# Logits in another bank, experts picked across a change of set, sums behind a tile: a two-layer expert FFN on one core

## The reference

```python
# first layer, one LoRA expert for each sequence
hidden_i = x @ wi.T + 2 * (x @ common_wi_a.T) @ common_wi_b.T + expert_lora(x, ids, wi_a, wi_b)
hidden_i = relu(hidden_i)
hidden_o = hidden_i @ wo.T + 2 * (hidden_i @ common_wo_a.T) @ common_wo_b.T + expert_lora(hidden_i, ids, wo_a, wo_b)
# second layer: the router looks at the mean over all tokens of a sequence
probs = softmax(hidden_o.mean(axis=1) @ gate_w)
top_w, top_i = top_k(probs, 2); top_w /= top_w.sum()
for e in range(8):
    y = gelu(hidden_o @ w1[e] + b1[e]) @ w2[e] + b2[e]
    out += combine[:, e] * y          # combine is top_w at top_i, else 0
return x + out
```

## Time and profile before

| what | us |
|---|---|
| median of three runs | 271.2 (271.2 to 271.35) |
| the profiled execution | 271.83 |
| its span, first to last instruction | 270.0 |
| TensorE busy | 262.4 |
| VectorE busy | 174.9 |
| ScalarE busy | 174.3 |
| GpSimd busy | 159.8 |

### The profile page before, as it was taken

The page is one execution under the profiler, slowest core; times in us unless marked ns, Lnnn a source line. Parts: engine busy times, 40 slices in busy tenths (PEclk is TensorE's granted clock), DMA queues, the critical chain, the costliest instruction groups (busy, mean ns, idle before and its releaser), DMA issues.

```text
span 270.0 us, 3606 instructions
## 1 busy us (share of the span) xinstructions
PE 262.4 (97%) x1150; PEld 211.8 (78%) x1150; DVE 174.9 (65%) x283; ACT 174.3 (65%) x279; POOL 159.8 (59%) x192
## 2 busy tenths in 40 slices
PE   7999999999979999999999999999999999999995
PEld 3668888887757888888888788888788888888883
DVE  1784767374699645657595696566865667665664
ACT  2747464554725459987986887677676776775650
POOL 2166998943666687799619999466356366331100
PEclk9999999999999999999999999999999999999999
DMA  5995120201023022112201122202012015000004
GB/s 183 350 385 187 39 78 0 83 1 39 0 71 111 16 78 78 21 60 78 80 1 27 51 78 80 64 13 81 24 56 78 33 47 195 0 0 2 0 1 155
DMA packets 11139, 19.76 MB, mean 73 GB/s; under 512 B 2000, under 2 KB 2256, under 8 KB 10992
## 3 DMA queue, kind: packets, MB, share of 16 engines
q1 hardware_dynamic: 10544, 18.61, 20.8%
q10 hardware_dynamic: 576, 0.92, 1.0%
HBM read 17.43 MB, written 2.10 MB: 72 GB/s over the span
## 4 chain that ended last, share of the span: by engine, by line
PE 90%; DVE 4%; issue 2%; ACT 1%; DMA 1%; SPq 1%; DVEq 0%; ACTq 0%
PE out_ps L732 15%; PE out_ps L733 15%; PE out_ps L736 15%; PE hid_ps L732 14%; PE hid_ps L733 13%; PE hid_ps L736 13%; DMA lora_first<-in_early 1%; PE hid_ps L776 1%; DVE hid_lo L1015 1%; PE hid_ps L772 1%; PE out_ps L850 1%; SPq L301 1%; ACT act_hi L628 1%; PE hid_ps L780 1%; DVE up_raw L999 1%
## 5 line engine op out<-in xcount | busy, mean ns | idle before, releaser
L406 POOL TENSOR_TENSOR up_lo<-up_raw,up_hi 128x512 fp32r<-128x512 f32 x41 | 53.0, 1312 | 41.9 <-ACT up_hi L559 41.7
L732 PE MATMUL out_ps<-hid_hi,down_hi 128*128 128x512 f32 x192 | 74.9, 390 | 0.0
L736 PE MATMUL out_ps<-hid_hi,down_lo 128*128 128x512 f32 x192 | 74.8, 389 | 0.0
L733 PE MATMUL out_ps<-hid_lo,down_hi 128*128 128x512 f32 x192 | 74.8, 389 | 0.0
L732 PE MATMUL hid_ps<-act_hi,up_hi 128*128 128x512 f32 x166 | 65.1, 392 | 0.5 <-DVE hid_lo L1015 0.3
L733 PE MATMUL hid_ps<-act_lo,up_hi 128*128 128x512 f32 x166 | 64.7, 390 | 0.0
L736 PE MATMUL hid_ps<-act_hi,up_lo 128*128 128x512 f32 x166 | 64.7, 390 | 0.0
L591 ACT ACTIVATE hid_ps<-hid_ps,bias_sb 128x512 f32<-128x512 f32 x64 | 42.2, 659 | 29.7 <-DVE hid_ps L1041 19.1
L1015 DVE SCALAR_TENSOR_TENSOR hid_lo<-hid_ps,mix,hid_hi 128x512 fp32r<-128x512 f32 x64 | 47.8, 747 | 18.7 <-ACT hid_hi L605 18.2
L412 POOL TENSOR_TENSOR down_lo<-down_raw,down_hi 128x512 fp32r<-128x512 f32 x24 | 32.1, 1338 | 41.5 <-ACT down_hi L569 41.3
L605 ACT ACTIVATE hid_hi<-hid_ps,mix 128x512 fp32r<-128x512 f32 x64 | 44.1, 689 | 4.6
(11 more groups left out here) (91 smaller groups left out, 236.3 us busy)
## 6 DMA issues: line engine op xcount, KB each, us to landing
up_raw<-in_w SPq DMA_DIRECT2D x16, 256.0 KB, 2.8
down_raw<-in_w SPq DMA_DIRECT2D x16, 256.0 KB, 2.6
lora_raw<-in_lora SPq DMA_DIRECT2D x10, 256.0 KB, 5.4
down_raw<-in_woT SPq DMA_DIRECT2D x8, 256.0 KB, 3.1
up_raw<-in_wiT SPq DMA_DIRECT2D x7, 256.0 KB, 3.8
outT<-x_sb SPq DMA_DIRECT2D x6, 256.0 KB, 3.3
x_sb<-in_xT SPq DMA_DIRECT2D x1, 1024.0 KB, 8.6
x_sb<-in_xT SPq DMA_DIRECT2D x1, 512.0 KB, 5.8
```

The costliest lines, as they stand in the source:

```text
L406: ins = eng.tensor_tensor(up_lo[:, n, cols], up_raw[:, n, cols], f32(up_hi[:, n, cols]), ALU.subtract)
L732: eng.matmul(out, w_h, a_h, start=start, stop=False, skip_group_check=onto)
L733: eng.matmul(out, w_h, a_l, start=False, stop=False, skip_group_check=onto)
L736: return eng.matmul(out, w_l, a_h, start=False, stop=stop, skip_group_check=onto)
```

## The change

No instruction is added or dropped on TensorE, and its order stays. What changes is where others stand, and which waits stand ahead of the logits:

- The logits of sequence 0 (set 5) go to bank 1 of `hid_ps` instead of bank 0. Bank 1 is free once `second_sum` has read it (`s_r2`); bank 0 was free once `hid_low(5, 0)` was done.
- `term_high` stands ahead of `hid_high(q, 0)`, and GpSimd makes the terms ahead of `lora_low(1, 4)`.
- `router_max` follows the reading of the logits at once, and `router_exp` stands in the middle of set 5.
- `router_softmax` and `router_first` come at the end of set 5, ahead of `hid_low(5, 3)`; `router_second` comes behind that.
- GpSimd waits in set 6 for both experts (`s_pick`) before it goes on; the four `token_sum` of sequence 0 move from set 5 to set 6, two ahead of `up_low(7)` and two behind, and `down_low(6)` behind them.
- `raw_high` moves from set 5 into set 6, behind `hid_high(6, 0)`; the two `sum_high` are put on either side of `hid_high(6, 2)`.

```diff
-    FIRST_AT = {6: 0, 11: 1}
+    FIRST_AT = {5: 0, 11: 1}
     SECOND_AT = {6: 0, 11: 1}
+    LOGITS_BANK = {5: 1, 10: 0}
...
@@ GpSimd
                 elif q == 4:
                     up_low(5)
                     down_low(4)
-                    after((s_down_lo, 5))
+                elif q == 5:
+                    logit_terms(0)
+                    term_low(0)
+                    after((s_term_lo, 1))
                     lora_low(1, 4)
-                elif q < N_COND - 1:
-                    if q in TOTAL_AT:
-                        logit_terms(TOTAL_AT[q])
-                        term_low(TOTAL_AT[q])
-                    up_low(q + 1)
-                    down_low(q)
-                    token_sums(q)
+                    up_low(6)
+                    down_low(5)
+                elif q == 6:
+
+                    eng.wait_ge(s_pick, TOP_K)
+                    token_sum(1, 0)
+                    token_sum(1, 1)
+                    up_low(7)
+                    token_sum(1, 2)
+                    token_sum(1, 3)
+                    down_low(6)
@@ ScalarE
                 if cond(q):
-                    hid_high(q, 0)
                     if q in LOGITS_AT:
                         term_high(LOGITS_AT[q])
+                    hid_high(q, 0)
+                    if q in EXP_AT:
+                        router_exp(EXP_AT[q])
...
+                    elif q == 6:
+                        raw_high(1, 0)
+                        raw_high(1, 1)
+                        up_high(7)
+                        hid_high(6, 1)
+                        down_high(6)
+                        sum_high(1, 0)
+                        hid_high(6, 2)
+                        sum_high(1, 1)
@@ TensorE, bank_free and router_logits
-                if bank == 0 and q - 1 in LOGITS_AT:
+                if q - 1 in LOGITS_AT and bank == LOGITS_BANK[q - 1]:
                     eng.wait_ge(s_read, LOGITS_AT[q - 1] + 1)
...
-                b = LOGITS_AT[q]
-                if b == 0:
+                b, bank = LOGITS_AT[q], LOGITS_BANK[q]
+
+                if bank == 0:
+                    eng.wait_ge(s_hid_lo, 4 * q + 1)
+                else:
                     eng.wait_ge(s_ones, 1)
-                eng.wait_ge(s_hid_lo, 4 * q + 1)
+                    eng.wait_ge(s_r2, sevens_before(q) + 1)
                 eng.wait_ge(s_term_hi, b + 1)
@@ VectorE
                     if q in LOGITS_AT:
-                        router_start(LOGITS_AT[q])
+
+                        router_start(q)
+                        router_max(LOGITS_AT[q])
                     tile_sum(q, 1)
                     for to in UP_FACTOR_AT.get(q, ()):
                         merge_up(to, hid_ps[:, 0, :])
                     tile_sum(q, 2)
-                    if q in LOGITS_AT:
-                        router_max(LOGITS_AT[q])
                     hid_low(q, 1)
                     merge_down(q, hid_ps[:, 0, :])
                     tile_sum(q, 3)
                     hid_low(q, 2)
+                    if q in FIRST_AT:
+                        router_softmax(FIRST_AT[q])
+                        router_first(FIRST_AT[q])
                     continue
                 if q > 1:
                     hid_low(q - 1, 3)
-                if q in FIRST_AT:
-                    router_softmax(FIRST_AT[q])
-                    router_first(FIRST_AT[q])
-                    router_second(FIRST_AT[q])
+                if q in SECOND_AT:
+                    router_second(SECOND_AT[q])
```

More of the change, by code:

```diff
@@ L107, in build @@
     EXP_AT = {5: 0, 11: 1}
-    FIRST_AT = {6: 0, 11: 1}
+    FIRST_AT = {5: 0, 11: 1}
     SECOND_AT = {6: 0, 11: 1}
+    LOGITS_BANK = {5: 1, 10: 0}
     MIX_B2_AT = {13: 0, 20: 1}
     READY_SEQ = [1, 0, 1]
-    RAW_HI_AT = {1: [(0, 0), (0, 1)], 5: [(1, 0), (1, 1)], 9: [(2, 0)], 10: [(2, 1)]}
+    RAW_HI_AT = {1: [(0, 0), (0, 1)], 9: [(2, 0)], 10: [(2, 1)]}
     RAW_LO_AT = {2: [(0, 0), (0, 1), (0, 2), (0, 3)], 6: [(1, 0), (1, 1), (1, 2), (1, 3)],
                  11: [(2, 0), (2, 1)], 12: [(2, 2), (2, 3)]}
-    SUM_AT = {1: [(0, 0), (0, 1)], 2: [(0, 2), (0, 3)], 5: [(1, 0), (1, 1), (1, 2), (1, 3)], 9: [(2, 0), (2, 1)], 10: [(2, 2), (2, 3)]}
-    SUM_HI_AT = {2: [(0, 0), (0, 1)], 6: [(1, 0), (1, 1)], 12: [(2, 0)], 13: [(2, 1)]}
+    SUM_AT = {1: [(0, 0), (0, 1)], 2: [(0, 2), (0, 3)], 9: [(2, 0), (2, 1)], 10: [(2, 2), (2, 3)]}
+    SUM_HI_AT = {2: [(0, 0), (0, 1)], 12: [(2, 0)], 13: [(2, 1)]}
     SUM_LO_AT = {3: [(0, 0), (0, 1), (0, 2), (0, 3)], 7: [(1, 0), (1, 1), (1, 2), (1, 3)], 13: [(2, 0), (2, 1)], 14: [(2, 2), (2, 3)]}
@@ L701, in _ @@
                         up_high(q + 2)
-                    if q in EXP_AT:
-                        router_exp(EXP_AT[q])
                     others(q)
@@ L884, in next_up_factor @@
                     eng.wait_ge(*free)
-                    if q in LOGITS_AT and seven(q):
-                        eng.wait_ge(s_read, LOGITS_AT[q] + 1)
                     up_factor(to, bank[:, 0:SW], bank[:, SW:2 * SW])
@@ L906, in router_logits @@
                     return
-                b = LOGITS_AT[q]
-                if b == 0:
+                b, bank = LOGITS_AT[q], LOGITS_BANK[q]
+                if bank == 0:
+                    eng.wait_ge(s_hid_lo, 4 * q + 1)
+                else:
                     eng.wait_ge(s_ones, 1)
-                eng.wait_ge(s_hid_lo, 4 * q + 1)
+                    eng.wait_ge(s_r2, sevens_before(q) + 1)
                 eng.wait_ge(s_term_hi, b + 1)
-                eng.matmul(hid_ps[:, 0, 0:KD * E], ones[:, :], term_hi[:, :, :].rearrange("p k e -> p (k e)"),
+                eng.matmul(hid_ps[:, bank, 0:KD * E], ones[:, :], term_hi[:, :, :].rearrange("p k e -> p (k e)"),
                            start=True, stop=True)
                 eng.wait_ge(s_term_lo, b + 1)
-                eng.matmul(hid_ps[:, 0, KD * E:2 * KD * E], ones[:, :], term_lo[:, :, :].rearrange("p k e -> p (k e)"),
+                eng.matmul(hid_ps[:, bank, KD * E:2 * KD * E], ones[:, :], term_lo[:, :, :].rearrange("p k e -> p (k e)"),
                            start=True, stop=True).then_inc(s_logit, 1)
@@ L1059, in _, with router_start @@
             max1, key1, max2, key2, inv, pair, inv_pair = (small[:, i:i + 1] for i in range(7))
-            def router_start(b):
+            def router_start(q):
+                b, bank = LOGITS_AT[q], LOGITS_BANK[q]
                 eng.wait_ge(s_logit, b + 1)
@@ L1064, in router_start @@
                     eng.wait_ge(s_exp, b)
-                eng.tensor_reduce(logit[:, :], hid_ps[:, 0, 0:2 * KD * E].rearrange("p (g e) -> p e g", e=E),
+                eng.tensor_reduce(logit[:, :], hid_ps[:, bank, 0:2 * KD * E].rearrange("p (g e) -> p e g", e=E),
                                   AX_X, ALU.add).then_inc(s_read, 1)
```

## The result

| | before | changed | ratio, 95% interval |
|---|---|---|---|
| median, six runs each, us | 271.61 (271.2 to 272.77) | 268.67 (267.93 to 269.93) | 0.9889 (0.9858 to 0.992) |
| profiled execution: span, us | 270.0 | 268.1 | |

The forecast was 268.1 us from 271.2, a ratio of 0.9886. The measured ratio is 0.9889, so the change takes 1.1% off, about 2.9 us of 271.6.

The account below looks back on a forecast made before the run. TensorE, busy 97% of the span, was taken as the bound, with four stalls of 3.30 us. Gains 0.40+0.71+1.80+0.39-0.15=3.15 us take the median from 271.2 to 268.1 us, range 267.6 to 269.5.

Parts of the forecast that it names:

- four stalls: TensorE, sets 5 and 6: before logits 0.40, up factor 0.71, down factor 1.80, tile 3 of set 6 0.39; together 3.30 us.
- Logits: Set 5: in bank 1 the logits no longer wait for hid_low(5,0), so TensorE gains 0.40 us.
- The cover of `router_max`: VectorE, set 5: the first tile sum waits for TensorE anyway, hiding router_max; without that, up to 0.6 us on VectorE.
- First expert and `hid_low(5,3)`: End of set 5: prob waits to 72.04, hid_low(5,3) ends at 73.55; the 0.71 us stall before set 7's up factor goes.
- the prediction's clock: Times in the profile before, run with the new order; the changed profile's times are 1.28 us later by its late start.
- The 0.2 to spare: Up factor of set 7: hid_low(5,3) ends at 73.55, TensorE comes at 73.80, leaving 0.2 us.
- Second expert: Set 6: picked without contention, merge_up(7) runs 74.6 to 75.3, wanted at 76.78; the 1.80 us stall goes.
- Merge of the down factor: VectorE, set 6: merge ends at 79.7, TensorE asks at 79.77; 0.15 us of the 0.39 before tile 3 stays.
- rival 1: Set 6: VectorE loses the shared port twice; stall 1.4 us instead of 0.15 before tile 3, 269.3 us; chance 0.15.
- the sign named for rival 1: Second mix or the raw_low after it over 1.2 us long, and a 1.4 us gap before tile 3 of set 6.
- Sums: Sets 6 to 8: sums' low parts come later but stay hidden; last act_lo ends near 92.0, about 1.8 us before set 8.
- Rival 3: Set 8 starts late, waiting for the sums' last act_lo; with one more wait of 1.28, 272.5 us; chance 0.04.

Follow-up runs that it names:

- the run of the split alone: Kernel before, with router_softmax and router_first moved to the end of set 5, GpSimd as before: stretch 77.12 against 77.81 us, ratio 0.9972.
- two sums pushed on: Changed kernel with the last two token_sum moved into set 7 behind down_low(7): stretch 77.85 us against 74.67, ratio to the kernel before 1.0048.
- experts with the rest: Kernel before, with experts picked across the change of set, GpSimd waiting for them and its sums in set 6: stretch 75.92 us, ratio 0.9914.

## Why the prediction was right

**The bound.** TensorE's work plus its four stalls: the stretch fell by 3.14 of the 3.30 that were read off, and all of it at the four places.

**Logits.** Forecast 0.40, read 0.37 in the changed kernel; 0.38 when the bank is undone. The cover of `router_max` held: the first tile sum started at 68.05, 0.1 behind the end of TensorE's product (67.56 and 0.39).

**First expert and `hid_low(5,3)`.** `prob` was to wait to 72.04, and waited to 73.35, which is 72.07 on the prediction's clock. `hid_low(5,3)` was to end at 73.55 and ended at 73.51 (74.79). TensorE came at 73.83 (75.11). The 0.2 to spare was 0.3, and one wait more on the port spends it: that is the run without the wait for the experts.

**Second expert.** `merge_up(7)` forecast 74.6 to 75.3, measured 74.62 to 75.31. TensorE's wish 76.78, measured 76.82. The stall of 1.80 is gone with 1.5 to spare. The run of the split alone shows that this needs GpSimd's rest: without it 0.79 stays.

**Merge of the down factor.** Forecast: first `mix` to 77.2, second at once, `raw_low` behind `up_low(7)`, merge done at 79.7, 0.15 left. Measured on the same clock: 77.34, 77.41, 79.13 and 79.73, with 0.14 left. This is where rival 1 would have decided. It did not come: in the nine traces with GpSimd's sums in set 6 the gap before tile 3 stays at or under 0.37. The forecast had no row, though, for the second `mix` getting in ahead of `up_low(7)`; it assumed it, and it was right by 0.01 us (78.55 against 78.56). Half of the sign named for rival 1 is no sign either: a `raw_low` of over 1.2 us is there (1.79), as the forecast's own wait for `up_low(7)` gives it. Only the gap tells the two apart.

**Sums.** The last `act_lo` was to end near 92.0 and ended at 92.45 (93.73). Set 8 began at 93.84 (95.12). So 1.4 of slack was left instead of the 1.8 that I gave. Rival 3's mechanism is real: with two sums pushed on, set 8 waited 3.2. Its price, counted as the wait alone, held in the three executions at full clock. In the profiled one the lower clock behind the wait added 2.9 us, which the prediction had nowhere. The forecast did not rest on this.

**What each part is worth.** Alone: logits 0.68, `raw_high` 0.62, experts with the rest 1.89, together 3.19 against 3.14 for all. Undone from the whole: 0.38, 0.26, 0.46 (the rest), 0.32 (the split), together 1.4. The parts add up when put in. The pieces taken out are in part smaller than those put in (the bank without the place of `router_max`, GpSimd's wait without the place of its sums), so the two sums can't be compared as they stand. `raw_high` is the same piece both ways, and there the rest of the change covers for it: 0.62 alone, 0.26 undone. The order of the sums around `up_low(7)` is worth nothing. The places of `router_exp`, of the terms and of `sum_high` were not run alone. No variant beat the changed kernel's stretch: the one with all sums ahead ties with it.

## What to carry to other kernels

When one engine is busy 97% of the span, read its own timeline for breaks in the pitch; add up the breaks, and that sum is the most that any reordering can give. Tiny operations that share a port with long ones can cost the long ones' length (1.00 instead of 0.23 here), so let the engine with the long ones wait, if it has the slack, and spend that slack knowingly. Here 1.4 us were left; the version that needed 3.2 more than there was gave back the whole gain, and in most of its executions 3 us more.

## What was not expected of the hardware

The price of a stall can be more than its length. TensorE's four stalls before the change, up to 1.70 long, left the granted clock at 1.0 in the profiled execution. The one of 3.0 us was followed by about 6 us at the lower level, which cost 2.9 us more. It is no fixed price: three of that kernel's ten executions kept full clock. Nor does a mean clock of 0.987 need such a stall. It is found in three of the 25 executions of the kernel before, measured beside it, and in four of the ten with the first expert behind `hid_low(5,3)`. Where those lost it no trace shows. That the stall drops the clock is what the rows suggest; it is not shown.

Which of two waiting operations gets the shared port next is worth 1.1 us to the one that loses, and it hangs on hundredths. In each of the eight traces in which GpSimd waits for the experts, the first `mix` waited for a sum and the second passed in the gap: in the changed kernel it starts at 78.55, `up_low(7)` at 78.56. The `raw_low` behind them, at 78.62, was too late and took 1.79. In the run without the wait for the experts `up_low(7)` started at 76.79, ahead of the second `mix`, which took 1.26; and this time `raw_low` (78.05) came ahead of GpSimd's next sum (78.07) and took its plain 0.68:

```profile
76.86 1.26 DVE L1120 TENSOR_TENSOR mix<-small 128x1 f32<-128x1 f32 x1
78.05 0.68 DVE L273 TENSOR_TENSOR act_lo<-y_sb,act_hi 128x512 fp32r<-128x512 f32 x1
```

```profile
78.07 3.61 POOL L428 TENSOR_TENSOR t_sum<-y_sb,t_sum 128x512 f32<-128x512 f32 x2
```

In all of them the one whose start comes first in the trace got the port, and VectorE never lost twice in a row. The rule of the Trainium skill ("SBUF — State Buffer", "Who interferes with whom"), that the issue order decides, agrees with these start times. The reading that I gave it in rival 1, that an operation whose semaphores are met counts as issued, does not: `up_high(7)` had been done since 78.33, and the second `mix` still went ahead of `up_low(7)`.
